# Expert numbers loaded two at a time behind a product, tiles gathered into other memory, and a count moved into the tile loop

## The reference, cut to what matters

```python
for j in range(C):
    residual = xf
    gate = (xf @ router_W[j] + router_b[j]) / TEMP
    biased = gate + gate_bias[j]
    _, ids = jax.lax.top_k(biased, TOPK)
    sel = (ids[:, :, None] == jnp.arange(E)[None, None, :]).any(axis=1)
    weights = jax.nn.softmax(jnp.where(sel, gate, -jnp.inf), axis=-1)
    h = jnp.einsum('nh,ehi->eni', xf, exp_Wup) + exp_bup[:, None, :]
    h = jax.nn.silu(jnp.einsum('eni,eij->enj', h, exp_Wg) + exp_bg[:, None, :]) * h
    eo = jnp.einsum('eni,eih->enh', h, exp_Wdown) + exp_bdown[:, None, :]
    combined = jnp.einsum('ne,enh->nh', weights, eo)
    s = (xf @ share_Wup + share_bup).reshape(-1, NS, I)
    s = jax.nn.silu(s @ share_Wg + share_bg) * s
    share_out = (s @ share_Wdown + share_bdown).sum(axis=1)
    z = combined + share_out
    y = residual + z
    y = y * jax.lax.rsqrt(jnp.mean(y * y, axis=-1, keepdims=True) + EPS) * norm_w[j]
    xf = y
```

## Time and profile before

| | |
|---|---|
| median of 3 runs | 2661.77 us (2660.13 to 2662.52) |
| the profiled execution | 2663.62 us, its span 2661.8 us, granted TensorE clock 0.974 |
| TensorE busy | 2485.6 us, 93% of the span |
| VectorE, ScalarE, GpSimd busy | 1942.4, 1781.3 and 1872.3 us |
| longest lines of the chain that ended last | L1814 7%, L1844 3%, L1688 3% of the span |

### The profile page before, as it was taken

One profiled execution on the slowest core, in us unless ns is written; L12 is line 12 of the kernel. 1 busy time (PEld: TensorE's weight loads), 2 busy tenths in 40 slices (PEclk: granted clock), 3 DMA queues, 4 the chain that ended last, 5 costly groups with the idle time before them and its releaser, 6 DMA issues. The chain is left out here.

```text
span 2661.8 us, 43897 instructions
## 1 busy us (share of the span) xinstructions
PE 2485.6 (93%) x12394; PEld 2067.2 (78%) x12394; DVE 1942.4 (73%) x4183; ACT 1781.3 (67%) x3874; POOL 1872.3 (70%) x1612
## 2 busy tenths in 40 slices
PE   6999999999999999999999999989997998879985
PEld 4888888888777788888888888877786887758874
DVE  7888888888887787888888888545675455864466
ACT  3788888888777788788788888833324664336662
POOL 3889889889878798898898999832263233554236
PEclk8999999999999999999999999989998999979997
DMA  3111212112111111111111110154244452225543
GB/s 77 38 39 48 45 39 44 37 29 55 38 37 30 28 25 29 29 29 31 29 29 30 25 23 20 43 172 137 96 155 149 151 182 83 72 103 185 175 143 121
DMA packets 168047, 189.60 MB, mean 71 GB/s; under 512 B 57524, under 2 KB 140346, under 8 KB 167303
## 3 DMA queue, kind: packets, MB, share of 16 engines
q1 hardware_dynamic: 154502, 152.96, 20.8%
q0 software_dynamic: 12288, 33.57, 3.9%
q10 hardware_dynamic: 1024, 0.26, 0.0%
HBM read 114.06 MB, written 81.17 MB: 73 GB/s over the span
## 5 line engine op out<-in xcount | busy, mean ns | idle before, releaser
L382 POOL TENSOR_TENSOR pl<-pr,ph 128x512 fp32r<-128x512 f32 (+1 forms) x1024 | 1301.9, 1294 | 182.1 <-ACT ph L872 164.8
L869 ACT ACTIVATE pr<-ps 128x512 f32<-128x512 f32 (+1 forms) x1152 | 664.2, 577 | 289.3 <-DVE ps L1058 144.3
L1145 DVE TENSOR_REDUCE part<-ps 128x1 f32<-128x512 f32 (+2 forms) x1152 | 697.9, 618 | 83.6 <-PE ps L583 67.8
L872 ACT ACTIVATE ph<-ps 128x512 fp32r<-128x512 f32 (+1 forms) x1152 | 663.5, 576 | 0.0
L583 PE MATMUL ps<-k_hi,q_parts 128*128 128x512 f32 (+3 forms) x1280 | 472.9, 370 | 25.7 <-DVE part L1145 10.6
L597 PE MATMUL ps<-q_row,k_lo 65*128 65x512 f32 (+1 forms) x1152 | 443.9, 385 | 0.0
L596 PE MATMUL ps<-q_parts,k_hi 128*128 128x512 f32 (+1 forms) x1152 | 442.9, 385 | 0.0
L583 PEld LDWEIGHTS ps<-k_hi,q_parts 128*128 128x128 f32 x1280 | 242.6, 190 | 90.4 <-DVE part L1145 19.4
L596 PEld LDWEIGHTS ps<-q_parts,k_hi 128*128 128x128 f32 x1152 | 217.3, 189 | 42.5
L597 PEld LDWEIGHTS ps<-q_row,k_lo 65*128 65x128 f32 x1152 | 217.2, 189 | 25.6
L1814 PE MATMUL ps<-exp_up,yy 128*128 x828 | 231.0, 414 | 2.5 <-ACT yy L2000 2.3
(11 more groups left out here) (286 smaller groups left out, 4405.1 us busy)
## 6 DMA issues: line engine op xcount, KB each, us to landing
work<-x_slots SPq DMA_DIRECT2D x138, 128.0 KB, 2.4
e_slots<-work SPq DMA_DIRECT2D x138, 128.0 KB, 1.8
y_latent<-y_sums SPq DMA_DIRECT2D x128, 128.0 KB, 2.4
rec<-recip_rows SPq DMA_DIRECT2D x127, 128.0 KB, 3.0
yg<-y_latent SPq DMA_DIRECT2D x30, 512.0 KB, 5.3
x_slots<-zero_rows SPq DMA_DIRECT2D x32, 276.0 KB, 3.8
acc_shared<-accw SPq DMA_DIRECT2D x14, 512.0 KB, 2.9
xcur<-acc_shared SPq DMA_DIRECT2D x12, 512.0 KB, 3.9
```

The lines of the kernel that those rows point to most:

```text
L382: eng.tensor_tensor(pl[:, s % RING, 0:w], pr[:, s % PR_RING, 0:w], f32(ph[:, s % RING, 0:w]), ALU.subtract).then_inc(sem, 1)
L869: act.activation(pr[:, s % PR_RING, 0:w], src, ACT.Exp).then_inc(S["probs"], 1)
L872: act.activation(ph[:, s % RING, 0:w], src, ACT.Exp).then_inc(S["probs_hi"], 1)
L1145: dve.tensor_reduce(dst, src[:, 0:w], AX.X, ALU.max).then_inc(S["max_read"], 1)
```

## The change

It has three parts that belong together.

1. `EXPERT_LOADS` now has a load every second tile, of two numbers (one at tile 26): 14 for the tiles below 27 and 21 from there on, 35 a round. On TensorE the loads move out of `turn_tile` to a function of their own, `tile_expert`, called behind the up product (and ahead of the transposes only for a round's first tile). On ScalarE they stay in `tile_seed`.
2. The tile buffers `xg` move to `accr[:, 0]`, which is free at the time, and the first load waits for the scatters alone. Rows that used to be put there go to `wk` instead (`acc_rows(8)`), and two waits are added for that: ScalarE's first activation of block 14, and a load of rows (13).
3. The count of a round's second group moves on TensorE from ahead of the first tile to behind the up product of the second tile, and to bank 7. VectorE's `take_counts` and `total_before` go behind the low part of the fourth tile. The wait for `counted` moves from the first tile's transposes to its down product.

```diff
-        xg = wk[:, 0:4 * D].rearrange("p (k d) -> p k d", d=D)
+        xg = F["accr"][:, 0]
...
+        def count_bank(g):
+
+            return T_BANK + 1 if g % 2 else COUNT_BANK
...
                 def load_tile(t):
                     c, s = t // TILES, t % TILES
                     if s == 0:
-                        last = LATE[0] if t else 8
                         sp.wait_ge(S[f"scattered{2 * c}"], DMA * 2 * JT)
-                        sp.wait_ge(S["gated"], 4 * last)
-                        sp.wait_ge(S["g_sum"], 2 * last)
...
                     elif r == 13:
-                        sp.wait_ge(S["stored0"], DMA * TPB)
+                        sp.wait_ge(S["t_x"], 2 * TILES)
...
-                        if k == 1 and r and r % QB == 0:
+                        if k == 1 and r % 8 == QB:
                             pe.wait_ge(S["counted"], r // QB)
...
                 def count(g):
 
-                    pe.wait_ge(S["gated"], 4 * min(QB * g + QB, LATE[0]))
+                    if g % 2 == 0:
+                        pe.wait_ge(S["gated"], 4 * (QB * g + QB))
...
-                    if r % QB == QB - 1:
+                    if r % 8 == QB - 1:
                         count(r // QB)
...
-                def turn_tile(t):
+                def tile_expert(t):
                     c, s = t // TILES, t % TILES
                     if s in (0, EARLY):
                         pe.wait_ge(S["tiles"], 2 * c + (2 if s else 1))
+                    expert.update(load_experts(mybir.EngineType.PE, t))
+
+                def turn_tile(t):
+                    c, s = t // TILES, t % TILES
                     if t >= 2:
                         pe.wait_ge(S["t_lo"], t - 1)
-                    if t == TILES:
-                        pe.wait_ge(S["gated"], 4 * LATE[0])
                     if s == 0:
-                        pe.wait_ge(S["counted"], 2 * c + 2)
-                    expert.update(load_experts(mybir.EngineType.PE, t))
+                        pe.wait_ge(S["gated"], 4 * (LATE[0] if c else 8))
...
                     else:
-                        pe.wait_ge(S["logits"], 8 * (t // TILES + 1))
                         pe.wait_ge(S["xt_lo"], 16 * (t // TILES + 1))
+                        pe.wait_ge(S["counted"], 2 * (t // TILES) + 2)
...
                     first, end = TILES * c, TILES * (c + 1)
+                    tile_expert(first)
                     turn_tile(first)
                     turn_tile(first + 1)
                     for t in range(first, end + 2):
                         if t < end:
                             tile_up(t)
+                        if t + 2 < end:
+                            tile_expert(t + 2)
                         if t == 0:
                             shared_down(7)
+                        if t == first + 1:
+                            count(2 * c + 1)
...
+                    if r == LATE[0]:
+                        act.wait_ge(S["stored0"], DMA * TPB)
...
-                        if t == first:
+                        if t == first + 1:
+                            take_counts(2 * c + 1)
                             total_before(2 * c + 1)
-                        if t == first + 1:
                             first_tiles(2 * c + 1)
...
-EXPERT_LOADS = {at: min(8, end - at) for start, end in ((0, EARLY), (EARLY, TILES)) for at in range(start, end, 8)}
+EXPERT_LOADS = {at: min(2, end - at) for start, end in ((0, EARLY), (EARLY, TILES)) for at in range(start, end, 2)}
```

More of the change, by code:

```diff
@@ L1356, in acc_rows @@
                 return xcur[:, r // QB, r % QB]
-            return {8: accr[:, 0], 9: accr[:, 1], 10: xcur[:, 1, 0], 11: xcur[:, 1, 1],
+            return {8: wk[:, 0:4 * D].rearrange("p (j d) -> p j d", d=D), 9: accr[:, 1], 10: xcur[:, 1, 0], 11: xcur[:, 1, 1],
                     12: xcur[:, 0, 2], 13: xcur[:, 0, 3], 14: xcur[:, 1, 2], 15: xcur[:, 1, 3]}[r]
@@ L1718, in count @@
                 def count(g):
-                    pe.wait_ge(S["gated"], 4 * min(QB * g + QB, LATE[0]))
+                    if g % 2 == 0:
+                        pe.wait_ge(S["gated"], 4 * (QB * g + QB))
                     pe.wait_ge(S["route"], ROUTE_STEPS * (QB * g + QB - 1) + 10)
                     mask = F["chosen"][:, g % 2].rearrange("p j e -> p (j e)")
-                    pe.matmul(ps[:, COUNT_BANK, 0:JT * E], W["before"][:, :], mask, start=True, stop=True)
-                    pe.matmul(ps[:, COUNT_BANK, JT * E:2 * JT * E], W["count"][:, 1:2].broadcast_to([P, P]), mask, start=True, stop=True).then_inc(S["counts"], 1)
+                    bank = count_bank(g)
+                    if g % 2:
+                        pe.wait_ge(S["logits"], QB * g + QB)
+                    pe.matmul(ps[:, bank, 0:JT * E], W["before"][:, :], mask, start=True, stop=True)
+                    pe.matmul(ps[:, bank, JT * E:2 * JT * E], W["count"][:, 1:2].broadcast_to([P, P]), mask, start=True, stop=True).then_inc(S["counts"], 1)
                 def make_shared():
@@ L2328, in take_counts @@
                     dve.wait_ge(S["counts"], g + 1)
-                    dve.tensor_copy(F["ranks"][:, :, :].rearrange("p a n -> p (a n)"), ps[:, COUNT_BANK, 0:2 * JT * E]).then_inc(S["counted"], 1)
+                    dve.tensor_copy(F["ranks"][:, :, :].rearrange("p a n -> p (a n)"), ps[:, count_bank(g), 0:2 * JT * E]).then_inc(S["counted"], 1)
                 def assigned(g, n, ins):
@@ L2611, in block_of @@
                         bias_lo()
-                    if r % QB == QB - 1:
+                    if r % 8 == QB - 1:
                         take_counts(r // QB)
-                    if r % 8 == QB - 1:
                         total_before(r // QB)
```

## The result

| | before | after |
|---|---|---|
| median of 5 runs each | 2661.77 us | 2643.82 us (2641.64 to 2647.49) |
| ratio after to before | | 0.9945 [0.9931, 0.9959] |
| the profiled execution, its span | 2663.62, 2661.8 us | 2641.64, 2639.9 us |

What follows compares the result with a forecast made beforehand. The expert stages were taken to run at TensorE's rate, 2.67 us a tile, with gaps from register loads. Terms −17.8 + 1.4 + 1.0 + 1.0 = −14.4 us gave 2647.4 us from the median 2661.77, range 2644 to 2656.

Steps and rivals of the forecast that it cites:

- Part 1: Expert stages, TensorE: removing loads of eight, dear at tiles 27, 35, 43, 51, 59 each round, gains 17.8 us.
- odd: Expert number table: eights starting at odd numbers, 27 and on, are dear; those at 0, 8 and 16 cheap.
- Part 2: Expert stages: 70 loads of two behind the up product on TensorE cost 0.02 us each, 1.4 us; bounds 0 and 11.
- Part 3: Seam into the first round: earlier tile loads gain 0; VectorE's later count leaves 0.45 us of delay in that round.
- Part 4: Seam into the second round: with the count moved, transposes wait only for the tile; first product 1.0 us earlier.
- Part 5: VectorE's count one tile later delays gating 1.75 us, shown at round two's tile 7; parts 3 to 5 cost 1.0 us.
- Part 6: Tile loads issued behind 512 KB loads: waits hidden by dear register loads come out, about 1.0 us; bounds 0 and 4.
- Rival C: Tile transfers become the bound: 0.8 us waits return at five places, growing to 1.5, 7.5 us, 2654; chance 0.13.

Runs made afterwards that it cites:

- experiment 1: Kernel before with only the register loads changed: pairs every second tile, on TensorE behind the up product; 2639.83 against 2657.90 us, 0.9931.
- experiment 3: Kernel before with loads of two every second tile, still ahead of the transposes on TensorE; 2644.10 us, 0.9950.
- experiment 4: Kernel before with loads at the old place, the late eights starting at multiples of eight (five numbers at 27 and 64); 2648.46 us, 0.9960.
- experiment 5: Kernel before with eights starting elsewhere, two kernels: 3, 11, 19, 30, 38, 46, 54 (2677.75 us); multiples of four and not of eight (2647.24 us).
- experiment 6: Kernel of experiment 1 with the old table of eights, so eights behind the up product; 2650.64 us against 2659.18 before, one run.
- experiment 2: Changed kernel with the loads of eight back at their old tiles, ahead of the transposes; 2660.80 us, 1.0008 of before.
- g4: Kernel before with only the 512 KB reloads moved ahead of the gathers and round 2's kept-row loads spread; 2653.68 against 2657.51 us, 0.9982.
- experiment 7: The changed kernel again, unchanged, on another chip; 2644.07 us against 2659.18 before, 0.9945.
- f3: Kernel before with eights starting at 3, 11, 19, 30, 38, 46 and 54, at the old place; 2677.75 us against 2659.18 before, single run.
- g2: Changed kernel with the second group's count, take_counts and total_before back where they were; 2642.67 us against 2657.51 before, 0.9939.

## Why the prediction was right

The time was forecast at 2647.4, with 2644 to 2656 as bounds. The median came to 2643.8, at the lower end of them and 0.2 us outside; the ratio, applied to the median before, gives 2647.1. From −14.4 us the ratio's −14.6 differs by nothing that can be measured, with an interval of −18.4 to −10.9. That the two agree to 0.2 us is in part luck. The loads alone gave −18.3 where parts 1 and 2 make −16.4, the late count cost more than forecast, and the disturbance by transfers came at other places and in other sizes. These errors cancel in part, and in the times of the whole kernel none of them is clear of the intervals. The mechanism, dear loads that go by where they start, was right and is shown by experiments 1, 3, 4 and 5. Term by term:

- **Part 1, −17.8.** Held. In the two profiles the ten dear places (each with the tile behind it) shrink by 17.3 us, and experiment 1 has −18.3 for the loads in all. The reason given for the price, position, was right; "odd" was too narrow (experiment 5). The 12.2 us of gaps hold a little of two eights that the prediction called cheap: the sixth gap of each round stands ahead of tile 8 (0.21 us, round 1) and tile 16 (0.20 us, round 2). For tile 16 it read round 1 alone (15: 2.74); round 2 has 15: 3.12.
- **Part 2, +1.4, bounds 0 and 11.** Too dear: nothing shows on TensorE in any of the five kernels with pairs behind the product, and 0.19 us beside idle time on ScalarE. The value is the lower bound, 0. The premise that cover behind the up product mattered was nearly idle: most pairs fit at the old place too (experiment 3), where an eight at a bad start doesn't, in either (experiments 5 and 6). The Trainium skill's rule ("Runtime: NRT & Kernel Launch", Instruction fetch mechanics) of some 200 ns a register, by which only the cover would differ, is near the 0.25 us per further number read from starts off a multiple of four; no run supports it at a multiple of four, where eight numbers stay hidden.
- **Part 3, 0 and +0.45.** The first product of round 1 stands 1.17 us earlier, but the last shared down product ahead of it already did by as much (2014.77 and 2013.60), so the seam gave 0. Of the 0.45 for VectorE at most 0.16 was seen: tiles 1–7 took 27.98 us and now 27.62, but 0.52 of that is the product of tile 7 (4.46, now 3.94), ahead of which the eight of tile 8 stood; tiles 1–6 took 23.52 and now 23.68.
- **Part 4, −1.0.** Held: last scatter (2377.20, now 2362.28) to first product went from 7.36 to 6.39 us.
- **Part 5, +1.55 in round 2.** Right in kind, too small: 2.14 (20.44, now 22.58), although the product of tile 7 gave back 0.23 as the eight of tile 8 went. It was placed at tile 7's gap; that gap stayed at 1.00, and a new one of 1.13 us stood ahead of the up product of tile 4 instead. Parts 3 to 5: 1.0 forecast, −0.96 − 0.36 + 2.14 = 0.8 read, and +2.1 [−0.3, +4.8] measured alone (experiment 2), which includes the transfers.
- **Part 6, +1.0.** A net term without a firm sign. The rows that I pointed to did not come back: round 1 waits 6.1 us for tile loads in two places, against 7.9 in four, and behind the first tile of round 2 they come to 4.7 us in the changed kernel's first profile and 6.0 in its second, against 5.1 before. Rival C with its 7.5 falls. But the disturbance is elsewhere and larger: at tile 45, up to 4.3 us over 2.67, where gathers meet a reload. It was 0.1 us in the changed kernel's first profile and 2.1 in its second, where the gathers began 1.9 us earlier (2142.10 for 2143.98) and met the reload sooner. In round 2 the product of tile 67 followed that of tile 59 by 28.60 us instead of 26.16. One wait in it had been hidden behind the dear load of tile 59: the four kernels with that load ahead of or behind the product (before, experiments 2 and 6, g4) read 60: 3.07 to 3.19, all others 3.66 to 4.04.

```profile
2537.53 0.35 PE L1811 MATMUL ps<-bias,pick 128*128 128x256 f32 x1 [0.99 <-issue]
```

The other wait, for the load of a tile, had not been hidden: it was 1.79 us before and 2.13 now. What it sets off is new.

```profile
2549.33 0.41 PE L1806 MATMUL ps<-ident,accr 128*128 128x128 f32 x2 [2.13 <-DMA accr<-x_slots]
2549.56 1.96 PE L1820 MATMUL ps<-exp_up,yy 128*128 x6
```

Behind it the granted clock of TensorE fell (a row by stage, same columns as above), and the product of tile 64 followed by 3.95 us instead of 2.67:

```profile
2549.60:2553.50 3.90, 3.90 (x19) 3.54 (x18) 0.85 (x2) 1.59 (x5) 0.71 (x1) 0.65 0.45 141
```

The second profile of the changed kernel has no such fall here (64: 2.67), and g4, with its dear loads, has one (64: 4.12). So these 1.3 us belong to the execution and not to the change.

- **Where the profiles differ by more.** Of the 4.0 us between the rounds 1.0 is part 4. The other 3.0 stand in the blocks stage, where the change only adds two waits (blocks 13 and 14) and moves the rows of one block. TensorE's first group of twelve shared up products in it, before and after:

```profile
2240.66 4.84 PE L1688 MATMUL ps<-xt_hi,share_up 128*128 128x512 f32 x12
```

```profile
2228.72 3.48 PE L1689 MATMUL ps<-xt_hi,share_up 128*128 128x512 f32 x12
```

The same twelve took 1.36 us longer before. The granted clock of the stretch was 0.60 before and 0.81 after (same columns as above, before then after), so part of it ran at the lower of the two levels:

```profile
2240.00:2246.00 6.00, 6.00 (x20) 4.72 (x19) 0.00 (x0) 1.05 (x2) 4.65 (x5) 0.60 0.36 106
```

```profile
2228.00:2233.00 5.00, 5.00 (x22) 4.03 (x21) 0.04 (x1) 1.28 (x2) 3.82 (x4) 0.81 0.36 107
```

The twelve at 2258.20 before took 4.50 us, those at 2244.91 after 2.91; with the 1.36 us these are 2.95 of the 3.0. It belongs to the execution: the second profile of the changed kernel (experiment 7) has 4.51 for the same twelve, at a granted clock of 0.62, where the first profile had 1.00:

```profile
2244.21 4.51 PE L1689 MATMUL ps<-xt_hi,share_up 128*128 128x512 f32 x12
```

That is why I set the sum beside the ratio and not beside the two spans.

Open are two things: what the late count costs in the whole kernel (its gap is shown, a difference of the times isn't), and what makes a load dear beyond its start (the seven at 20, and a start that leaves one when divided by four, which no eight here has).

## What to carry to other kernels

Before cutting a load of register numbers into small ones, look where it starts: eight numbers starting at a multiple of four were nearly as free as pairs. When a serial stage is freed of its gaps, read which other work was hidden beside each gap (here gathers next to a 512 KB reload), and move that too: together it gave −27 us, where the loads alone gave −18. Moving work later so that one engine starts earlier pays only if the engine that takes the work has idle time there.

## What the runs showed of the hardware

- A TENSOR_LOAD of eight int32 numbers costs TensorE 0 to 0.3 us beside 0.22 us of transposes where it starts at a multiple of four of the table (once 0.46, at tile 16 of round 2 before, where a pair shows 0.24 too), and 1.3 to 1.95 us at its tile where it leaves two or three when divided by four (tiles 30 and 11). Seven numbers from 20 on cost 0.78. ScalarE shows the same: 0.42 us of idle time at tile 16, 1.53 at tile 35, 1.96 at tile 11 of f3.
- Pairs behind the product cost nothing on TensorE at any start, odd ones too; ahead of the transposes they cost nothing from tile 27 to 44, 0.1 to 0.3 us at tiles 16 and 59, and once 0.7 at tile 63.
- Behind six products an eight at a bad start still shows 0.5 to 0.9 us at its tile (0.24 at tile 27 of round 2, behind a long wait), and 0.36 at the next.
- Gathered rows came 6.9 us after the first gather's start with a 512 KB reload issued 1.8 us behind it (experiment 1), 6.0 with 2.1 (the changed kernel's second profile: 2142.10, 2144.24, 2148.10), and within 4.4 with 2.5 (its first). Over all kernels: 5.8 to 6.9 us where the reload came 1.4 to 2.1 us behind (six profiles), at most 4.2 to 4.9 where it came 2.5 us or more behind, or not at all (eight profiles).
- The same twelve products of 128x512 took 2.91 and 4.51 us in two executions of one kernel, with a granted clock of 1.00 and 0.62.
- A gap can cost more than its length, and not in every execution. Behind a wait of 2.8 us for the load of a tile the six up products of tile 23 of round 2 took 2.91 us in g2 (granted clock 0.50) and 1.67 in experiment 1 (1.00), with the same wait.
